# Layer 0 of a feature-crossing tower: six steps of 128 rows, the left-over products of two units in one step, both turns of a tile in one body

## The reference

```python
z0 = jnp.einsum('bid,bjd->bdij', e, e).reshape(B, D, 39 * 39)
cur0 = jax.nn.relu(jnp.einsum('bdk,kl->bld', z0, W0))     # 128 outputs
next_h, direct0 = jnp.split(cur0, 2, axis=1)              # 64 and 64
z1 = jnp.einsum('bid,bjd->bdij', e, next_h).reshape(B, D, 39 * 64)
cur1 = jax.nn.relu(jnp.einsum('bdk,kl->bld', z1, W1))
z = jnp.sum(jnp.concatenate([direct0, cur1], axis=1), axis=-1)
h = jnp.concatenate([z, dense_ctx], axis=1)
...
y = h @ W_top3                                            # after two relu layers on h
```

## Time and profile before

| | |
|---|---|
| time, median of 3 runs (lowest, highest) | 1476.11 us (1474.81, 1478.93) |
| profiled execution, span | 1510.1 us (the times list no figure of its own for it) |
| PE busy, of its span | 1434.6 us, 95% |
| DVE busy | 1393.3 us, 92% |
| POOL busy (600 gathers) | 939.0 us, 62% |
| ACT busy | 825.2 us, 55% |
| DMA moved | 293.08 MB |

### The profile page before, as it was taken

How to read it: one execution, slowest core, us unless ns; L and a number is a source line. 1 busy time by engine, 2 the same in 40 slices (tenths; PEclk the granted TensorE clock), 3 DMA queues, 4 the chain that set the end, 5 groups by cost and what they waited for, 6 DMA issues and landing times.

```text
span 1510.1 us, 15015 instructions
## 1 busy us (share of the span) xinstructions
PE 1434.6 (95%) x4458; PEld 794.5 (53%) x4458; DVE 1393.3 (92%) x1253; ACT 825.2 (55%) x897; POOL 939.0 (62%) x604
## 2 busy tenths in 40 slices
PE   3179999999999999999999999999999999999999
PEld 2145555555555555555555555555555555555556
DVE  2179999999999999999999999999999999999993
ACT  0155555655655555655655555655655555655555
POOL 7638888868687786868687786868687780000000
PEclk7589999999999999999999999999999999999999
DMA  5069989999989899999989999899998998898510
GB/s 150 6 160 203 227 216 218 206 220 212 221 198 222 206 217 214 208 223 201 220 203 216 214 212 220 208 213 203 212 216 223 212 210 216 204 222 207 170 35 1
DMA packets 137289, 293.08 MB, mean 194 GB/s; under 512 B 37646, under 2 KB 62878, under 8 KB 137080
## 3 DMA queue, kind: packets, MB, share of 16 engines
q1 hardware_dynamic: 102642, 278.48, 77.2%
q0 software_dynamic: 19200, 4.95, 2.9%
q10 hardware_dynamic: 15366, 8.70, 2.1%
HBM read 284.08 MB, written 7.87 MB: 193 GB/s over the span
## 4 chain that ended last, share of the span: by engine, by line
PE 90%; DVE 4%; issue 2%; another core or an unknown queue 2%; ACT 0%; DMA 0%; DVEq 0%; SPq 0%
PE psB L493 42%; PE psA L493 14%; PE psB L511 7%; PE psB L514 6%; PE psB L518 6%; PE psA L501 2%; PE psA L511 2%; PE psA L514 2%; PE psA L518 2%; PE psB L501 2%; DVE z L902 1%; PE psA L485 1%; DVE z_lo L911 1%; DVE z_split L902 1%
## 5 line engine op out<-in xcount | busy, mean ns | idle before, releaser
L472 POOL DMA_INDIRECT emb<-in_tbl,ids_all x600 | 938.8, 1565 | 309.7 <-issue 178.9
L493 PE MATMUL psB<-z,w 128*128 128x512 f32 x1544 | 690.1, 593 | 5.3 <-DVE z L902 5.3
L767 ACT ACTIVATE z_hi<-z_split 128x1024 fp32r<-128x1024 f32 (+1 forms) x286 | 301.4, 1057 | 464.9 <-DVE z_split L902 372.4
L493 PEld LDWEIGHTS psB<-z,w 128*128 128x128 f32 x1544 | 292.4, 190 | 362.7 <-issue 346.0
L902 DVE TENSOR_TENSOR z<-h_quad,x_lay 128x1024 f32<-128x1024 f32 x354 | 420.5, 1218 | 7.4 <-PE psB L493 5.4
L911 DVE TENSOR_TENSOR z_lo<-z_split,z_hi 128x1024 fp32r<-128x1024 f32 (+1 forms) x286 | 349.3, 1221 | 6.3 <-ACT z_hi L767 3.2
L902 DVE TENSOR_TENSOR z_split<-h_quad,x_lay 128x1024 f32<-128x1024 f32 x222 | 268.4, 1221 | 0.0
L720 ACT ACTIVATE h_quad<-psA 32x1024 f32<-32x1024 f32 x248 | 251.7, 1015 | 6.1 <-DVE feat_side L987 2.4
L493 PE MATMUL psA<-z,w 126*128 126x512 f32 x512 | 241.9, 594 | 0.0
L511 PE MATMUL psB<-z_hi,w_hi 128*128 128x512 f32 x444 | 157.7, 436 | 0.0
L493 PEld LDWEIGHTS psA<-z,w 126*128 126x128 f32 x512 | 97.3, 190 | 98.4 <-issue 92.7
(11 more groups left out here) (113 smaller groups left out, 862.5 us busy)
## 6 DMA issues: line engine op xcount, KB each, us to landing
x_lay<-x_rows SPq DMA_DIRECT2D x1152, 128.0 KB
x_more<-x_rows SPq DMA_DIRECT2D x62, 504.0 KB
bases<-x_rows SPq DMA_DIRECT2D x62, 468.0 KB
x_lay<-x_rows SPq DMA_DIRECT2D x64, 256.0 KB
x_ring<-x_rows SPq DMA_DIRECT2D x31, 504.0 KB
emb<-in_tbl,ids_all POOLq DMA_INDIRECT x600
x_last<-x_rows SPq DMA_DIRECT2D x64, 128.0 KB
x_rows<-x_side ACTq DMA_DIRECT2D x58, 120.0 KB
```

Of the source, the lines that this page charges most:

```text
L472: nc.gpsimd.indirect_dma_start(emb[t % 2][:, f * D:(f + 1) * D], None, tables[f], bass.IndirectOffsetOnAxis(ids_all[:, t, f:f + 1], 0)).th ...
L493: mm = nc.tensor.matmul(ps[:, cs], w[0:k, :], z[WHOLE_NO[place] % NZ][0:k, cs], start=first, stop=last)
L767: nc.scalar.activation(z_hi[n % NS][0:k, 0:cols], z_split[n % NS][0:k, 0:cols], ACT.Copy).then_inc(z_hi_made, 1)
```

## The change

Layer 0's six whole steps get 128 rows in place of 126: 117 as before (each of 39 fields three times) and 11 more, every second field from a first one on (`EXTRA_BASE`, `EXTRA_MORE`). 762 products are covered, 18 left over. Those are done for two units at once: the left-over step of an even unit u has four groups of 32 partitions, 18 rows each, for the two column halves of unit u and of unit u + 1 (`left_a`, `left_b`, `left_product`, four matmuls). Odd units have six steps of layer 0, and their `psA` half is begun by this step. Units 0 and 1 have a left-over step each, with two groups. For this the odd unit of a tile must be turned and stored one body earlier, so both turns stand in the even body, units u + 2 at s2 and u + 3 at s11 (body 0: s9 and s15), and go to two banks of the same half of `psA`. The ten left-over loads in each body (`load_halves`) become eight in each odd body (`load_left`), issued behind the last `x_lay` of the unit; each shifted copy has a second DMA. At the start DVE makes the shifted copies in three pairs of copies in place of one long copy, and clears `left_a` and `left_b`.

```diff
-EXTRA = (63, 72)
-HALF_A = ((11, 49), (29, 15))
-HALF_B = ((29, 10), (1, 39), (8, 15))
+EXTRAS = P - ROWS0
+EXTRA_BASE = (0, 1)
+EXTRA_MORE = (19, 20, 21)
+LEFT = 18
+LEFT_A, LEFT_B = 4, 22
+GROUP = P // 4
...
+def left_units(u):
+
+    return (u,) if u < 2 else (u, u + 1) if u % 2 == 0 else ()
+
+
+def steps0(u):
+
+    return STEPS0 if left_units(u) else STEPS0 - 1
+
+
+def left_groups(u):
+
+    return [(v, c) for v in left_units(u) for c in range(C // BANK)]
...
+def turns(u):
+
+    if u % 2 or u + 2 >= UNITS:
+        return ()
+    return ((u + 2, 9), (u + 3, 15)) if u == 0 else ((u + 2, 2), (u + 3, 11))
...
+        def turned(u):
+            if u < 2:
+                return half(psA, u)[:, 0:BANK]
+            return half(psA, 0)[:, u % 2 * BANK:(u % 2 + 1) * BANK]
...
-            def load_halves(u):
-                if u >= 1:
-                    sp.wait_ge(z_made, at0(u - 1, STEPS0 - 1) + 1)
-                for dst, loaded, runs in ((half_a, half_a_loaded, HALF_A), (half_b, half_b_loaded, HALF_B)):
-                    p = 0
-                    for f, rows in runs:
-                        src = x_rows[u, f:f + rows, :]
-                        for n in range(2):
-                            sp.dma_start(dst[n * HROWS + p:n * HROWS + p + rows, :],
-                                         src[:, n * BANK:(n + 1) * BANK]).then_inc(loaded, 16)
-                        p += rows
+                sp.dma_start(more[t][0:ROWS0, :], ring(u, SH * t)).then_inc(more_loaded[t], 16)
+                sp.dma_start(more[t][ROWS0:P, :], every_second(u, EXTRA_MORE[t], EXTRAS, 0, C)).then_inc(more_loaded[t], 16)
+
+            def load_left(u):
+                if u == 1:
+                    sp.wait_ge(z_made, at0(0, STEPS0 - 1) + 1)
+                else:
+                    sp.wait_ge(z_made, at0(max(u - 2, 1), STEPS0 - 1) + 1)
+                for k, (v, c) in enumerate(left_groups(u)):
+                    rows = slice(k * GROUP, k * GROUP + LEFT)
+                    sp.dma_start(left_a[rows, :], every_second(v, LEFT_A, LEFT, c * BANK, BANK)).then_inc(left_loaded, 16)
+                    sp.dma_start(left_b[rows, :], every_second(v, LEFT_B, LEFT, c * BANK, BANK)).then_inc(left_loaded, 16)
...
+                if u % 2 and u + 1 < UNITS:
+                    sp.wait_ge(x_stored, 32 * (u + 2) + 32)
+                    load_left(u + 1)
...
+            def left_product(u):
+
+                place = at0(u, STEPS0 - 1)
+                pe.wait_ge(z_made, place + 1)
+                if u >= 2:
+                    pe.wait_ge(relu0_done, u)
+                for k, (v, c) in enumerate(left_groups(u)):
+                    rows = slice(k * GROUP, k * GROUP + LEFT)
+                    mm = nc.tensor.matmul(half(psA, v)[:, c * BANK:(c + 1) * BANK], w0[rows, ORDER0.index(STEPS0 - 1), :],
+                                          z[WHOLE_NO[place] % NZ][rows, 0:BANK], start=v > u, stop=v == u)
                 mm.then_inc(z_used, 1)
...
+                first = s == 0 and len(left_units(u)) > 0
+                last = s == STEPS0 - 2 and not left_units(u)
+                if first:
+                    pe.wait_ge(x_kept, u + len(left_units(u)))
                 if s == STEPS0 - 1:
-                    half_product(half(psA, u), at0(u, s), w0[:, ORDER0.index(s), :], True)
+                    left_product(u)
...
-                    if s == turn_before(u) and u + 2 < UNITS:
-                        turn_x(u + 2)
+                    for v, t in turns(u):
+                        if s == t:
+                            turn_x(v)
...
-                    if s == turn_before(u) - 2 and u + 2 < UNITS:
-                        spread_x(u + 2)
-                    if s == turn_before(u) + 2 and u + 2 < UNITS:
-                        keep_x(u + 2)
+                    for v, t in turns(u):
+                        if s == t - (2 if v % 2 == 0 else 1):
+                            spread_x(v)
+                        if s == t + 2:
+                            keep_x(v)
...
+            nc.vector.memset(left_a[:, :], 0.0).then_inc(left_cleared, 1)
+            nc.vector.memset(left_b[:, :], 0.0).then_inc(left_cleared, 1)
...
             spread_base(0)
-            nc.vector.tensor_copy(in_groups(ring_spread), ring_of(0, RING_ROWS // SH)).then_inc(part_spread, 1)
+            spread_more(0)
             spread_base(1)
-            spread_half(0, HALF_A)
-            spread_half(1, HALF_B)
+            spread_more(1)
+            spread_more(2)
+            spread_left(0, LEFT_A)
+            spread_left(1, LEFT_B)
```

More of the change, by code:

```diff
@@ L106, in at0, with last0 @@
 def at0(u, s):
-    return s if u == 0 else STEPS0 + STEPS * (u - 1) + after(u - 1)[s] + 1 + s
+    return s if u == 0 else FIRST1[u - 1] + after(u - 1)[s] + 1 + s
 def at1(u, s):
-    return STEPS0 + STEPS * u + s + sum(a < s for a in after(u))
+    return FIRST1[u] + s + sum(a < s for a in after(u))
+def last0(u):
+    return at0(u, steps0(u) - 1)
+FIRST1 = [steps0(0) + sum(STEPS1 + len(after(v)) for v in range(u)) for u in range(UNITS)]
 def split1(u):
@@ L445, in _ @@
             load_more(1, 2)
-            load_halves(1)
+            load_left(1)
             for u in range(UNITS):
@@ L583, in turn_part @@
                 if n == 4:
-                    pe.wait_ge(ring_kept, 1)
-                rows = ROWS if n < 5 else HROWS
+                    pe.wait_ge(more_kept, 1)
+                rows = P if n < 5 else GROUP
                 for d in range(DH):
@@ L697, in keep_x @@
                     act.wait_ge(x_stored, 32 * u)
-                nc.scalar.activation(x_side[:, :], half(psA, u)[0:2 * RING, 0:BANK], ACT.Copy).then_inc(x_kept, 1)
+                nc.scalar.activation(x_side[:, :], turned(u)[0:2 * RING, :], ACT.Copy).then_inc(x_kept, 1)
                 if u >= 3:
@@ L917, in step0 @@
                         dve.wait_ge(part_kept, 6)
+                        dve.wait_ge(left_cleared, 2)
                     else:
-                        dve.wait_ge(half_a_loaded, 32 * len(HALF_A) * u)
-                        dve.wait_ge(half_b_loaded, 32 * len(HALF_B) * u)
-                    make(at0(u, s), half_a, half_b)
+                        dve.wait_ge(left_loaded, 32 * sum(len(left_groups(v)) for v in range(1, u + 1)))
+                    make(at0(u, s), left_a, left_b)
                     return
@@ L1088, in _, with ring_of, every_second @@
             dve.wait_ge(hot_kept, hot_no(HOT_TILES, 0))
-            def ring_of(first, groups):
-                x = emb_spread[:, :, first:first + groups]
-                return bass.AP(x.tensor, x.offset, [list(x.ap[0]), [RING, DH], [1, groups], [1, SH]])
+            def ring_of(first):
+                x = emb_spread[:, :, first:first + F]
+                return bass.AP(x.tensor, x.offset, [list(x.ap[0]), [RING, DH], [1, F], [1, SH]])
+            def every_second(first, rows):
+                x = emb_spread[:, :, first:first + 1]
+                return bass.AP(x.tensor, x.offset, [list(x.ap[0]), [RING, DH], [2, rows]])
             def in_groups(x):
@@ L1215, in rows @@
         if s == STEPS0 - 1:
-            one = [(f + n) % F for f, k in HALF_A for n in range(k)]
-            two = [(f + n) % F for f, k in HALF_B for n in range(k)]
-            return one, two
+            return [LEFT_A + 2 * g for g in range(LEFT)], [(LEFT_B + 2 * g) % F for g in range(LEFT)]
         c, t = PRODUCTS0[s]
-        one = [(p // SH + TURNED[c]) % F if p < ROWS0 else ring(EXTRA[c] + p - ROWS0) for p in range(ROWS)]
-        two = [ring(3 * SH * t + p) for p in range(ROWS)]
+        one = [(p // SH + TURNED[c]) % F if p < ROWS0 else EXTRA_BASE[c] + 2 * (p - ROWS0) for p in range(P)]
+        two = [ring(3 * SH * t + p) if p < ROWS0 else (EXTRA_MORE[t] + 2 * (p - ROWS0)) % F for p in range(P)]
         return one, two
@@ L1231 @@
                 covered.add(pair)
-                for q in ((p,) if s < STEPS0 - 1 else (p, p + HROWS)):
+                for q in ((p,) if s < STEPS0 - 1 else range(p, P, GROUP)):
                     w0_a[q, ORDER0.index(s)] = W0[one * F + two]
```

120 lines of the change are left out of this document (55 added, 65 removed).

## The result

The changed kernel takes **1513.51 us** (median of 4 runs, 1513.24 to 1514.63) where the kernel before takes 1475.81 beside it: 1.0248 times the time, 95% interval 1.0234 to 1.0263. That is 37.7 us more; 33.1 were forecast. The profiled execution took 1513.26, with a span of 1511.5, so here trace and time can be read side by side.

A forecast was written before the change was run, and what follows sets the result against it. TensorE was taken to set the pace, with VectorE 5% behind. To 1476.1 us it added 30.8 for 14 pairs and 3.2 for bodies 0 and 1, less 0.9 for body 30: 1509.2 us, range 1493 to 1526.

The forecast's parts named there:

- TensorE sets the pace, and VectorE is right behind it: Steady loop body of 42.47 us: TensorE busy for 42.47, VectorE for 40.48, 5% behind.
- The path through the second turn: Even body: from T, the turn's start, z_hi comes at T + 3.13, s15 at T + 8.20; loss 1.60 us.
- What the odd body adds: Up to z_lo of s9, VectorE's lateness of 2.51 leaves TensorE 2.2 us late; 30.8 us over 14 pairs.
- The left-over step adds nothing for its four groups: Left-over step of even units: four matmuls side by side cost no more than two, so nothing added.
- Bodies 0 and 1: Unit 3's turn in body 0 holds ScalarE, making z_hi late in body 1: +3.2 us, bounds 0 and 4.3.
- Body 30: Body without a turn, losing only its left-over step: -0.9 us.
- Start-up and left-over loads: Extra copies at the start cost 0, at most 1 us; the eight left-over loads are hidden, VectorE not waiting.
- the faster one (A): ScalarE works on during its issues or the copy comes early enough; TensorE's 12.9 us are won: 1463 or 1466, chance 0.10.

The follow-up runs named there:

- the kernel with the quiet turn: The changed kernel with the odd unit's turn moved on TensorE from ahead of s11 to right behind s9, where ScalarE is idle: 1469.55 us, 0.9952 times before.

## Why the prediction was right

The direction, the mechanism and the time held: 1509.2 was forecast and 1513.5 measured, inside the range. Point by point:

- **TensorE sets the pace, and VectorE is right behind it.** Right, and VectorE is nearer than the 5% that the prediction names. That is an even body; in the odd body behind it, VectorE is busy for all of the 42.50 us, as PE is (the window of 739.60 above), and so can hardly make up for lateness. After the change both are idle part of the time, since each waits for the late z_hi.
- **The path through the second turn.** Right almost to the hundredth: z_hi at T + 3.13 forecast and measured, z_lo at T + 4.22 forecast and measured, the end of z_lo of s14 at T + 7.74 against T + 7.72. s15 starts at T + 8.34 in place of 8.20. PE's waits on the way are shorter than forecast, 0.87, 0.07 and 0.62 where 1.1, 0.2 and 0.9 were named, in part since PE needs longer in between: the turn takes 0.43 on PE in place of 0.35, and a pair of products that follows a wait 0.57 in place of 0.46. That the issues hold ScalarE was the deciding premise; the runs with issues added to the kernel before bear it out.
- **What the odd body adds.** Right: PE takes z_lo of s9 at T + 40.83 (755.90 - 715.07), before at T + 38.58 (771.42 - 732.84), so it is 2.25 late where 2.2 was forecast. It waits 0.52 there, where about 0.8 was named. But even to even the pair is 2.49 longer, not 2.2: the prediction put nothing behind this point, and 0.24 arise there, nearly all of it in the left-over step.
- **The left-over step adds nothing for its four groups.** The run with two groups says so. This is all the same the term that was mis-sized, by 0.21 a pair: the step and the half step behind it take 2.13, not 1.92. The 1.92 came from two steps of one shape, 64 rows each, one behind the other, of which the second cost 0.86; after the change an 18-row step precedes a 64-row step, and each costs what the half step costs alone, 1.06. The prediction took the step out at the price of 0.86, rightly (the half step that is left alone takes 1.06), but kept the price of a like neighbour for the one that stays. That the unlike neighbour is the reason is argued from these rows, not shown by a run of its own. The Trainium skill (TensorE: Matmul & The Clock Gate, Part 3), by its packing factor of 3.07x, gave some 4 us for four groups as an estimate; 15 x 0.21 = 3.2 is close in size, but two groups cost the same as four, so it is not their number that costs.
- **Bodies 0 and 1.** PE waits 3.11 for z_hi there, 3.2 forecast. PE reaches the first z_lo of body 1's layer 0 at 124.73, and at 121.86 and 121.57 in the two variants of the kernel before, whose start is untouched: +3.0. A single execution places this only to about 1.5 us (123.22 to 126.18 in the five kernels with this start, 124.7 on the mean). The profile of the kernel before reaches the place at 157.57: it was 36 us late by then, and less these its span of 1510.1 is 1474, as in the timed runs (1473 to 1477). So carrying the loop's cost over to the median was sound, but the price of bodies 0 and 1 was read in a start unlike that of the timed runs, and that it came out there too is in part luck.
- **Body 30.** 40.30 before, 39.35 after: -0.95, -0.9 forecast.
- **Start-up and left-over loads.** No wait for `left_a` or `left_b`; the start costs nothing that can be told from the +3.0.

Summed by the trace: 14 x 2.49 + 3.0 - 0.95 = 36.9, against 37.7 by the medians and 33.1 forecast. Of the difference of 4.1 in the pairs the dearer left-over step is 2.9 (14 x 0.21); the rest is 0.05 a pair up to z_lo of s9 (2.25 late, not 2.2) and 0.03 behind it. That s15 starts 0.14 later than forecast does not enter, since PE still has to wait 0.52 at z_lo of s9.

Of the rivals, the faster one (A) needed ScalarE to go on with z_hi while its issues run. Where z_hi stands right behind them and its product is ready, it does not, in any run. About half of the 12.9 us that A promised were there to be had, though not that way: with the turn where ScalarE is idle the pair is 0.64 shorter than before, and the kernel 0.5% faster. By the terms above that is 14 x 0.64 + 0.95 - 3.0 = 6.9 us; 6.7 were measured. The limit of what is left is not settled: in the kernel with the quiet turn z_lo of s9 in the odd body is ready just as PE wants it (at 735.27; PE starts on it at 735.33), so less work on PE alone may bring little more. No run tries that.

## What to carry to other kernels

An engine that hands a value to a busy engine must be on time for that engine, not for the one at the end of the line: TensorE had 2 us of slack for z_hi, VectorE next to none, and 0.95 us of waiting on VectorE came out as 0.74 on the total of each pair. Before a copy with DMA issues is moved onto an in-order engine, look at what stands next behind it in the order, and at where the engine is idle: the same turn cost 3.1 us a pair more ahead of s11 than 3.4 us earlier. When steps are merged, price what stays anew, beside the neighbour that it then has.

## What the runs showed of the hardware

- **A DMA issue holds back what is behind it, not what is ahead.** With the issues behind both z_hi in ScalarE's program, the first ran from 705.94 while z_hi of s13 ran from 705.81, and the second from 706.85 while z_hi of s14 did; the relu behind them started at 707.81, when both were done, so the 1.73 us of issues cost ScalarE nothing. With the issues ahead, z_hi started at 718.20, 0.10 after they ended at 718.10; so it did, 0.10 after, in all 14 even bodies of the changed kernel and of both kernels with added issues. The Trainium skill (Advanced Engine Details and Errata, Sequencer Loop) says that other engine instructions can be read and queued while a control instruction executes. Here that did not let a ready activation behind the issues start before they ended; the activations ahead of them in the order ran on beside them.
- **Two small steps in a row cost less on TensorE when they were alike.** Two 64-row steps take 1.92, an 18-row step and a 64-row step behind it 2.13, with four groups of 18 rows, and 2.12 with two. So it is not the number of groups; whether it is the change of layout or the 18 rows as such is not shown.
